# A mixture-of-experts stage with tiles of 256 rows instead of 128, and its inner layer computed transposed

## What is computed

```python
def _moe(h, gate_w, w1, w2):                 # t: 8224 tokens x 256
    logits = t @ gate_w
    top_v, top_i = jax.lax.top_k(logits, TOP_K)          # 2 of 8 experts
    gates = jax.nn.softmax(top_v, axis=-1)
    combine = jnp.zeros((T, N_EXP), t.dtype).at[jnp.arange(T)[:, None], top_i].add(gates)
    hid = jax.nn.silu(jnp.einsum('td,edh->teh', t, w1))  # 256 -> 512
    ye = jnp.einsum('teh,ehd->ted', hid, w2)             # 512 -> 256
    out = jnp.einsum('te,ted->td', combine, ye)
```

## Time and profile before

| | us |
|---|---|
| median of 3 runs | 3233.44 |
| lowest and highest | 3223.12, 3235.12 |
| the profiled execution | 3228.84 |
| its span in the profile | 3227.0 |
| mean granted TensorE clock | 0.968 of full speed |

### The profile page before, as it was taken

One profiled execution on the slowest core, in us unless ns is written; L12 is line 12 of the kernel. 1 busy time (PEld: TensorE's weight loads), 2 busy tenths in 40 slices (PEclk: granted clock), 3 DMA queues, 4 the chain that ended last, 5 costly groups with the idle time before them and its releaser, 6 DMA issues. The chain is left out here.

```text
span 3227.0 us, 67632 instructions
## 1 busy us (share of the span) xinstructions
PE 2987.7 (93%) x21936; PEld 2303.3 (71%) x21937; DVE 2108.6 (65%) x5558; ACT 1431.1 (44%) x2884; POOL 1150.4 (36%) x973
## 2 busy tenths in 40 slices
PE   3999999999999999999859999999999992999998
PEld 1677777777777777777537777777777761999997
DVE  4677777767777777776526777777777765444443
ACT  0444554554454455445404444444444442444443
POOL 3333433443443344344311222222222224444444
PEclk7999999999999999999969999999999995999999
DMA  3333442443343344234221111111111101444444
GB/s 82 92 87 73 101 99 66 95 104 75 81 104 88 72 101 103 64 92 104 49 51 31 37 49 42 36 52 41 37 52 39 39 31 46 73 75 78 76 78 67
DMA packets 161128, 223.14 MB, mean 69 GB/s; under 512 B 30305, under 2 KB 125730, under 8 KB 161074
## 3 DMA queue, kind: packets, MB, share of 16 engines
q1 hardware_dynamic: 135138, 187.50, 23.2%
q0 software_dynamic: 25936, 34.95, 6.9%
HBM read 125.26 MB, written 97.08 MB: 69 GB/s over the span
## 5 line engine op out<-in xcount | busy, mean ns | idle before, releaser
L66 POOL TENSOR_TENSOR vrn<-vsm,inv_root 128x16 f32<-128x16 f32 x64 | 247.1, 3862 | 282.1 <-DVE vsm L844 282.1
L673 ACT ACTIVATE R<-psA 128x1024 f32<-128x1024 f32 x256 | 262.5, 1025 | 167.9 <-PE psA L1158 164.3
L865 DVE TENSOR_TENSOR PR<-R 128x1024 f32<-128x1024 f32 x256 | 320.9, 1254 | 0.0
L2528 POOL DMA_INDIRECT out_rows<-e_y,e_dest x137 | 213.4, 1557 | 290.7 <-DMA out_rows<-e_y,e_dest 205.8
L1907 DVE TENSOR_REDUCE m_nm<-psC 128x4 f32<-128x1028 f32 (+1 forms) x256 | 239.4, 958 | 99.5 <-PE psC L2184 99.4
L1173 PE MATMUL psA<-PR,V 128*64 128x258 f32 x2048 | 283.2, 397 | 0.0
L1785 ACT ACTIVATE m_PT<-psC 128x770 f32<-128x770 f32 x256 | 194.1, 811 | 150.5 <-PE psC L2210 150.5
L678 ACT ACTIVATE oTs<-psA 128x258 f32<-128x258 f32 x256 | 99.2, 387 | 357.9 <-PE psA L1173 352.3
L1218 PE MATMUL psA<-wout,OT 128*128 128x256 f32 x1024 | 244.5, 382 | 0.4 <-DVE OT L907 0.4
L1704 POOL DMA_INDIRECT xg<-tn,idx x124 | 122.4, 987 | 335.5 <-DMA xg<-tn,idx 225.4
L1218 PEld LDWEIGHTS psA<-wout,OT 128*128 128x128 f32 x1024 | 188.5, 191 | 24.6 <-DVE OT L907 0.7
(11 more groups left out here) (423 smaller groups left out, 7774.4 us busy)
## 6 DMA issues: line engine op xcount, KB each, us to landing
ks<-kparts SPq DMA_DIRECT2D x256, 128.0 KB, 3.2
qs<-qparts SPq DMA_DIRECT2D x256, 128.0 KB, 3.6
e_x<-xg SPq DMA_DIRECT2D x143, 129.0 KB
xraw<-in_x SPq DMA_DIRECT2D x66, 256.0 KB
qparts<-qh SPq DMA_DIRECT2D x128, 128.0 KB, 2.4
kparts<-kh SPq DMA_DIRECT2D x64, 128.0 KB, 2.5
kparts<-kl SPq DMA_DIRECT2D x64, 128.0 KB, 2.4
qparts<-ql SPq DMA_DIRECT2D x64, 128.0 KB, 2.4
```

Of the source, the lines that this page charges most:

```text
L66: return pool.tensor_tensor(out, x, e.to_broadcast(list(out.shape)), ALU.pow)
L673: act.activation(R[:, p % 2].rearrange("p a t n -> p t a n"), ps[:, 0:2, :].rearrange("p t (a n) -> p t a n", a=2), ACT.Relu).then_inc(rel ...
L865: dve.tensor_tensor(PR[:, p % 2, :, :, 0:L], R[:, p % 2], R[:, p % 2], ALU.mult).then_inc(prob_done, 1)
L2528: pool.indirect_dma_start(out, bass.IndirectOffsetOnAxis(ap=dest[:, b % XD:b % XD + 1], axis=0), y[:, b % XD], None, compute_op=ALU.add).t ...
```

## The change

Tiles have 256 rows, in two halves h of 128. `n_tiles` becomes 73: 9, 8, 9, 7, 7, 13, 9 and 7 used tiles, 69 in all, and 4 idle ones.

- `hidden` makes the inner layer transposed. A 128x128 piece of w1 is the stationary side and the 256 turned rows stream past, so that the result has the 512 inner columns on the partitions, as `output` needs it; `turn_s` is gone. 24 matmuls of 256 columns take the place of two times six of 512.
- A stationary operand isn't read at an address from a register here; so ACT and DVE copy the tile's expert's `w1l` and `w1h` (128x1024 each) into `e_w` for each tile (`low_weights`, `high_weights`).
- Silu is two instructions of 512; `e_sh` and `e_sl` are made from `e_S` in SBUF, 1024 elements a partition. `take` makes two multiplications.
- `add_rows` issues two indirect adds for a tile, h = 0 on `added0` and h = 1 on `added1`. Before the first of them it waits until both adds of the tile before have landed; before the second it waits for the first only in tile 0, in the last tile of an expert and in idle tiles (`until`).
- 16 writes of 128 rows of zeros behind the experts' rows instead of 8, and 32 spare-row writes at the start of `latent_attention` instead of 16. The tables are shorter (80 entries instead of 144).

```diff
-    v.n_tiles = 2 * v.groups * TOKT + NEXP - 1
+    v.n_tiles = -(-((2 * tokens + NEXP * (TILE - 1)) // TILE - 1) // 4) * 4 + 1
...
-                sp.dma_start(v.xg[bass.ds(r, P)], v.zeros[:]).then_inc(cleared, 16)
+                for h in range(TILE // P):
+                    sp.dma_start(v.xg[bass.ds(sp.snap(r + h * P), P)], v.zeros[:, h]).then_inc(cleared, 16)
...
-            dve.tensor_scalar(v.tile_wait[:, 1:n_tab], until[:, 1:n_tab], 16.0, None, ALU.max)
+            dve.scalar_tensor_tensor(v.tile_wait[:, 0:n_tab - 1], other[:, 0:n_tab - 1], 16.0, begun[:, 0:n_tab - 1],
+                                     ALU.mult, ALU.add)
...
             def add_rows(b, n):
-                added, beside = (added1, added0) if b % 2 else (added0, added1)
+                pool.wait_ge(y_done, HT * n + 1)
+                until = 16
                 if b:
-                    until = pool.value_load(v.tile_wait[0:1, bass.ds(n, 1)], min_val=16, max_val=8 * n_tiles + 16)
-                pool.wait_ge(y_done, n + 1)
-                if b >= 2:
-                    pool.wait_ge(added, 8 * (n - b % 2))
+                    until = pool.value_load(v.tile_wait[0:1, bass.ds(n, 1)], min_val=16, max_val=16 * n_tiles)
+                    pool.wait_ge(added0, 16 * n)
+                    pool.wait_ge(added1, 16 * n)
                     pool.sem_inc(y_free, 1)
-                if b:
-                    pool.wait_ge(beside, until)
-                    pool.sem_inc(y_clear, 1)
-                pool.indirect_dma_start(out, ... y[:, b % XD], None, compute_op=ALU.add).then_inc(added, 16)
+                for h, added in enumerate((added0, added1)):
+                    if h:
+                        pool.wait_ge(y_done, HT * n + 2)
+                        pool.wait_ge(added0, until)
+                        pool.sem_inc(y_step, 1)
+                    pool.indirect_dma_start(out, ... y[:, b % XD, h], None, compute_op=ALU.add).then_inc(added, 16)
...
             def s_high(d, n):
-                act.activation(sh[:, d].rearrange("p k n -> p (k n)"), ps[:, SB + d, :], ACT.Copy).then_inc(s_hi, 1)
+                act.wait_ge(silu_done, 2 * n)
+                act.activation(sh[:, d], S[:, d], ACT.Copy).then_inc(s_hi, 1)
+            def low_weights(d, e, before):
+                if before is not None:
+                    act.wait_ge(hid_done, before)
+                act.activation(w1[:, d, 1], part(v.w1l, e, 0, KT * HID).bitcast(F32), ACT.Copy).then_inc(w1_low, 1)
...
             def take(b, n):
                 dve.wait_ge(w2_done, n)
                 dve.wait_ge(y_free, n)
...
+            def high_weights(d, e, before):
+                if before is not None:
+                    dve.wait_ge(hid_done, before)
+                dve.tensor_copy(w1[:, d, 0], part(v.w1h, e, 0, KT * HID).bitcast(F32)).then_inc(w1_high, 1)
...
                 for d in range(XD):
-                    take(d, XD * i + d + 1)
                     s_low((d + 1) % 2, XD * i + d + 2)
+                    take(d, XD * i + d + 1)
+                    dve.wait_ge(y_done, HT * (XD * i + d) + 1)
                     x_low(d + 3, XD * i + d + 4)
+                    high_weights((d + 1) % 2, es[d], 2 * XD * i + 2 * d + 4)
...
-            def hidden(d, e):
-                for k in range(KT):
-                    pe.matmul(ps[:, HB + d, :], xh[:, d, k], part(v.w1h, e, c, HID), start=k == 0, stop=False)
...
+            def hidden(d, n):
+                pe.wait_ge(x_lo, n)
+                pe.wait_ge(w1_high, n)
+                pe.wait_ge(w1_low, n)
                 for m in range(MT):
-                    last = pe.transpose(ps[:, SB + d, m * P:(m + 1) * P], S[:, d, m * P:(m + 1) * P], v.identd[:])
-                last.then_inc(s_T, 1)
+                    rows = ps[:, HB + 2 * d + m // 2, m % 2 * TILE:(m % 2 + 1) * TILE]
+                    for k in range(KT):
+                        c = k * HID + m * P
+                        pe.matmul(rows, w1[:, d, 0, c:c + P], xh[:, d, k], start=k == 0, stop=False)
+                        pe.matmul(rows, w1[:, d, 1, c:c + P], xh[:, d, k], start=False, stop=False)
+                        last = pe.matmul(rows, w1[:, d, 0, c:c + P], xl[:, d, k], start=False, stop=k == KT - 1)
```

More of the change, by code:

```diff
@@ new lines, in experts @@
+        x = sbuf(nc, ctx, "e_x", [P, XD, HT, ROW])
+        meta = sbuf(nc, ctx, "e_meta", [P, XD, HT, 2])
+        xh = sbuf(nc, ctx, "e_xh", [P, 2, KT, TILE], F32R)
+        xl = sbuf(nc, ctx, "e_xl", [P, 2, KT, TILE], F32R)
+        S = sbuf(nc, ctx, "e_S", [P, 2, MT, TILE])
+        sh = sbuf(nc, ctx, "e_sh", [P, 2, MT, TILE], F32R)
+        sl = sbuf(nc, ctx, "e_sl", [P, 2, MT, TILE], F32R)
+        w1 = sbuf(nc, ctx, "e_w1", [P, 2, 2, KT * HID], F32R)
+        y = sbuf(nc, ctx, "e_y", [P, XD, HT, MODEL])
@@ L2492, in experts, with registers, read_experts, known @@
         block = ctx.enter_context(nc.Block())
         n_tiles = v.n_tiles
[L2494 to L2495 removed]
+        top = v.xg.shape[0] - TILE
+        def registers(eng, name):
+            return [eng.alloc_register(f"expert_{name}{n}") for n in range(XD)]
+        def read_experts(eng, regs, at):
+            eng.load(regs, v.tile_e[0:1, bass.ds(at, XD)])
+        def known(eng, reg):
+            return eng.snap(reg, min_val=0, max_val=NEXP - 1)
+        def part(w, e, c, n):
+            return w[:, bass.ds(e, 1), c:c + n].rearrange("p a n -> p (a n)")
@@ new lines, in output @@
+            def output(d, e, lows):
+                pe.wait_ge(s_lo, lows)
+                for h in range(HT):
+                    rows = slice(h * P, (h + 1) * P)
+                    sums = ps[:, YB + d, h * MODEL:(h + 1) * MODEL]
+                    for m in range(MT):
+                        c = m * MODEL
+                        pe.matmul(sums, sh[:, d, m, rows], part(v.w2h, e, c, MODEL), start=m == 0, stop=False)
+                        pe.matmul(sums, sh[:, d, m, rows], part(v.w2l, e, c, MODEL), start=False, stop=False)
+                        last = pe.matmul(sums, sl[:, d, m, rows], part(v.w2h, e, c, MODEL), start=False,
+                                         stop=m == MT - 1)
```

206 lines of the change are left out of this document (90 added, 116 removed).

## The result

| | before | after |
|---|---|---|
| median, us (4 runs each) | 3229.13 | 3314.94 |
| lowest and highest | 3223.12, 3235.12 | 3309.59, 3320.05 |
| the profiled execution | 3228.84 | 3309.59 |
| its span | 3227.0 | 3307.6 |

The changed kernel is slower by 2.7%: the ratio is 1.0266, with a 95% interval from 1.0237 to 1.0294. Predicted were 3281 us, in a range of 3248 to 3325. (The table has one run of the kernel before more than the part ahead of the prediction, 3224.82, so its median is lower.)

A forecast was written before the change was run, and what follows sets the result against it. POOL's paired adds were taken to bound the expert stage instead of PE: 60 x 6.6 + 13 x 9.5 = 519.5 us, +41.8, plus 10.0 at the start, on 3228.84 gives 3281 us, range 3248 to 3325.

The forecast's parts named there:

- the chain of the pairs on POOL: Expert tiles: issue 1.55, gap 0.17 to 0.30, second add's issue and landing 4.75; 6.47 to 6.60 us, above PE's 5.96.
- The rivals with PE as the bound: Expert tiles: adds land sooner, PE's 5.96 us a tile rules; 3207 us (faster, chance 0.10) or 3226 (tie, 0.10).
- second rival: POOL's issue stretched by DVE's copy of `w1h`, +0.6 us a tile, pairs at 7.2, 3325 us; chance 0.18.
- The case with the chance of 0.62: Expert tiles: POOL's pairs of adds set the pace at 6.3 to 6.9 us; chance 0.62.
- the three signs that were to show the prediction wrong: Tile-to-tile starts under 6 us, issues longer than 1.6 us as a rule, or PE's inner-layer pitch not 0.115.
- The pair's period: POOL's adds in 60 paired tiles: 6.6 us each, the upper end of the two gaps.
- the timeline I gave DVE: `take` begins as POOL starts a tile; `x_low` and the copy follow 2.0 to 2.7 us in, within the second issue.
- The thirteen serial tiles: Tile 0, each expert's last tile and four idle tiles: halves one after the other, 2 x 4.75 = 9.5 us each.
- PE's pace: PE per 256-row tile: 48 matmuls of 0.115 and four transposes of 0.11, 5.96 us; saving 35 us if PE stays bound.
- The start: Ahead of the first add: zero writes and first tile together +10 us, bounds 8 to 15.
- The writes of zeros: SP's eight more writes ahead of the experts: 4 to 9 us on the path, taken as 4.5.
- the first tile: First transposes to first add, with PE at a reduced clock: +4.4 to +6.3 us, taken as 5.5.

The follow-up runs named there:

- Experiment 1: Changed kernel, but within an expert a half's add waits only for the same half of the tile before: 3232.08 us, ratio 1.0018.
- experiment 3: Changed kernel with `e_sl` made by a plain copy of `e_S` instead of a subtraction (wrong low part): 3300.99 us, ratio 1.0238.
- experiment 8: Changed kernel with the copy of `w1h` cut to 32 columns from tile 2 on (wrong output): 3297.04 us in one run.
- experiment 2: Changed kernel with DVE's copy of `w1h` moved ahead of `take` and behind the `e_sl` subtraction: 3300.80 us, ratio 1.0236.
- experiment 4: Kernel before (128-row tiles) with the pairs' waiting rule alone: even tiles' adds wait for all earlier landings, odd ones follow directly: 3232.63 us, ratio 1.0026.
- experiment 10: Changed kernel with POOL's increment of `y_free` moved from ahead of a tile's first issue to between its two issues: 3307.89 us, ratio 1.0254.
- experiment 9: Changed kernel with experiment 1's waiting, POOL's `load_experts` subtractions after its scatters, one zero write per expert, DVE's subtractions paced by scatters: 3219.12 us, ratio 0.9984.

## Why the prediction was right, and where its sizes were off

**The bound.** PE loses its lead to the chain of the pairs on POOL, PE waits for `e_xl` and `take` for POOL: as predicted. Experiment 1 takes the chain away and with it nearly the whole loss. The rivals with PE as the bound needed the next tile to start 4.1 to 4.25 us after a second issue's start. It was 4.5 at best (3.7 of landing and 0.8 of hand-over, which the prediction read as one from the earlier trace rows), and 5.2 in the backlog.

**How right.** The time lies in the range, but near the 3325 of the second rival (stretched issues, chance 0.18) and not near 3281. The case with the chance of 0.62 had pairs at 6.3 to 6.9 us, and they took 7.09 in the mean. Two of the three signs that were to show the prediction wrong came: issues are longer than 1.6 us as a rule in the backlog (1.65 and 2.17), and the inner layer's pitch isn't 0.115. Starts alternate between 1.96 and 5.2 us there, not 1.8 and 4.8.

**The pair's period** is the term that was too small: 60 tiles took 425 us, 7.09 each, where the sum has 6.6. These 29 us are all that lies between the sum, 3280.6, and the profiled execution, 3309.6, as the other terms cancel (partly by luck, see the start); the median is 5 us above that. 6.6 was right until the backlog. In it, 0.6 us come from the held second issue and 0.1 from the first. The prediction had that as its second rival, with the right price (7.2 a tile) and the wrong culprit: by it the copy of `w1h` stretches the issue. The copy falls within the first issue and costs 0.10; it is the subtraction of `e_sl`, in progress at the start of the second, that costs 0.62 (experiments 1, 3 and 8, and the issues of 2; that run's time has another bound beside it). The step that failed is the timeline I gave DVE, in which `take` begins as POOL starts a tile. `y_free` lets it begin some 0.65 us earlier, and `e_sl`, which the sum has only as DVE's time, came into the second issue.

**The thirteen serial tiles** took 123 us, 9.5 each, as predicted.

**PE's pace.** A tile takes PE 6.15 us where it isn't held (70 us for 592 of 52 matmuls a tile), not 5.96: the pitch of the inner layer is 0.120, not 0.115. It costs nothing in the changed kernel, where POOL sets the pace. It is why experiment 1 comes out level: 73 x 6.15 = 449 us against the 470 of before save 21 us, not 35, and the later first add and the serial adds at the end take them back.

**The start.** The writes of zeros cost 4.2 (4.5 predicted) and the first tile 4.0 (5.5). `load_experts`, which I costed at nothing, cost 7.9 us. With shorter tables DVE begins its last run of subtractions 13.1 us into it (2685.04 to 2698.14) instead of 25.2, among POOL's scatters instead of behind them:

```profile
2716.77 3.48 DVE L2376 TENSOR_TENSOR w1l<-w1raw,w1h 128x1024 fp32r<-128x1024 f32 x3
```

This is the start of that run before; the last scatter had been issued at 2716.59. That a scatter takes longer beside such a subtraction was in the same group, and I used it for the loop alone. By experiment 4's trace the kernel before meets such a hold in some executions, so that a part of these 7.9 us may hang on which execution was profiled. All of the start together is 16.8 us where the sum has 10.

The shorter stages ahead, -6.5 us, hide this in the sum, and that is luck. They do the same work in both kernels, and the stage's first instruction comes between 2685.04 (the changed kernel's trace) and 2695.72 us in all the traces of this case.

**Open.** Why a short or shortened issue in the backlog mostly lands later than ahead of it, by 0.2 us in the mean and up to 0.8, and so gives back a part of what experiments 3, 8 and 10 win. The loads of `e_x` beside it are the likeliest cause, but it isn't shown. Also open is why a run of nine subtractions held a scatter to its end, and a run of two and one of five did not.

## What to carry to other kernels

Where adds in DRAM must not overlap, write the chain down as start to start, landing and hand-over, and compare it with the bound engine's period for the same rows: a saving on the engine is worth only what lies above the chain. Waiting for the same half of the tile before, instead of for both halves, is as safe within an expert and was worth 80 us here. And look at what DVE has in progress at the moment when POOL issues an indirect DMA: most of what is left of a large operation between SBUF tensors is added to the issue. Another order on DVE can avoid it, but then look at what it puts on PE's way: in experiment 2 it made a chain of 6.80 us.

## What the runs showed of the hardware

- **DVE's subtraction with two SBUF inputs holds POOL's indirect issue that begins within it.** 0.92 us left: the issue is 0.81 longer (experiment 1); 0.74 left: 0.62 longer (3067.69); 0.34 left: 0.21 longer. That is what is left, less 0.11 to 0.13. One that begins after the issue does not: at 2810.76 an `e_sl` started 0.38 us into an issue of 1.55. The Trainium skill (SBUF — State Buffer, section SBUF: two separate sides) has the pair of ports that DVE and GpSimd share as an exclusive lock for a whole instruction, taken by whoever starts first, with an operation of two SBUF inputs contending only against a GpSimd operation that reads SBUF. The rows agree, if an indirect issue counts as one that reads. The same section, where it tells who interferes with whom, has a probe in which a `tensor_tensor` did not stall a DMA, and infers that writing descriptors needs only the write side of the pair. Here the subtraction, a TENSOR_TENSOR, does hold the issue, and the measurement decides.
- **The copy of `w1h` does the same:** 0.60 us left, 0.47 longer (experiment 1); 0.44 left, 0.31 longer (experiment 10). Where it begins within an issue it adds 0.10. By the same section's trap for DMAs issued from POOL, the descriptors can't be written for the length of such a copy, 0.6 us here. The runs show that only for what was in progress at the start of the issue.
- **Back-to-back subtractions can hold POOL for a whole run of them:** 9.76 us for a scatter that takes 0.97, 11.68 for a subtraction that takes 2.36. Not always: two scatters that began 0.17 us into a run of two and a run of five took 1.90 (experiment 9), and one that began 0.18 us into a run of nine took 10.98 (experiment 1).
